# Taking the tiles of a mixture-of-experts layer in pairs, with half-row products of two tiles next to each other

## The reference, cut to what matters

```python
logits = xn2 @ w_gate                                   # 1152 x 8
top_vals, top_idx = jax.lax.top_k(logits, 2)
gates = jax.nn.softmax(top_vals, axis=-1)
...
h = jax.nn.gelu(xn2 @ w1 + bb1, approximate=False)      # 192 -> 768, per expert
return (acc + g[:, None] * (h @ w2 + bb2), None)        # 768 -> 192, weighted by the gate
...
return x + moe_out.reshape(Bx, Nx, C)
```

## Time and profile before

| | us |
|---|---|
| median of 3 runs (lowest, highest) | 360.93 (359.34, 362.2) |
| the profiled execution | 360.52 |
| its span, first to last instruction | 358.7 |
| transposes of tile 4, start | 267.20 |
| transposes of tile 19, start | 340.80 |
| mean granted TensorE clock | 0.974 |

### The profile page before, as it was taken

How to read it: one execution, slowest core, us unless ns; L and a number is a source line. 1 busy time by engine, 2 the same in 40 slices (tenths; PEclk the granted TensorE clock), 3 DMA queues, 4 the chain that set the end, 5 groups by cost and what they waited for, 6 DMA issues and landing times.

```text
span 358.7 us, 7680 instructions
## 1 busy us (share of the span) xinstructions
PE 328.8 (92%) x2651; PEld 284.8 (79%) x2651; DVE 209.2 (58%) x580; ACT 188.9 (53%) x505; POOL 84.3 (24%) x85
## 2 busy tenths in 40 slices
PE   8999997999799899999998888999899999989990
PEld 6977785787588888978997777788798998979890
DVE  1738995698988744453847785885333334332441
ACT  1064516946559177675757786223554455534450
POOL 9410002000000111010001000112164555645642
PEclk9999999899899999999999999996999999999997
DMA  8970000000000594911834222222122333223322
GB/s 268 354 232 0 3 0 1 0 2 0 0 2 0 153 319 122 261 47 48 243 118 108 60 80 92 68 55 76 49 38 43 53 54 54 38 43 55 63 31 25
DMA packets 23698, 29.18 MB, mean 81 GB/s; under 512 B 6010, under 2 KB 18762, under 8 KB 23658
## 3 DMA queue, kind: packets, MB, share of 16 engines
q1 hardware_dynamic: 19770, 23.85, 22.4%
q0 software_dynamic: 3888, 4.81, 8.3%
HBM read 23.54 MB, written 5.11 MB: 80 GB/s over the span
## 4 chain that ended last, share of the span: by engine, by line
PE 44%; DVE 15%; DMA 12%; ACT 12%; issue 11%; POOL 2%; DVEq 1%; POOLq 1%; ACTq 0%
DMA out<-ffn 11%; PE banks L1318 7%; PE banks L1348 7%; PE banks L1319 6%; PE banks L1564 3%; PE banks L1415 3%; PE banks L1547 2%; PE banks L1389 2%; PE banks L1459 2%; PE banks L1390 2%; PE banks L1471 2%; ACT patch L842 1%; POOL rs L635 1%; DVE st L974 1%; ACT xh L718 1%
## 5 line engine op out<-in xcount | busy, mean ns | idle before, releaser
L635 POOL TENSOR_TENSOR rs<-va,consts 96x6 f32<-96x6 f32 (+1 forms) x16 | 17.4, 1087 | 199.5 <-DVE va L980 101.3
L1564 PE MATMUL banks<-arena,ffn 128*128 x240 | 42.9, 329 | 0.0
L667 POOL DMA_INDIRECT out<-ffn x20 | 32.3, 1617 | 44.1 <-DVE ffn L1275 37.4
L1564 PEld LDWEIGHTS banks<-arena,ffn 128*128 128x128 f32 x240 | 38.5, 190 | 0.6 <-issue 0.2
L906 ACT ACTIVATE ffn<-banks,chans 128x128 f32<-128x128 f32 x21 | 9.6, 458 | 52.9 <-PE banks L1537 52.9
L657 POOL DMA_INDIRECT vs<-xh_scratch,ffn x21 | 21.9, 1041 | 17.6 <-DVE ffn L1242 9.3
L1415 PE MATMUL banks<-rvw,ffn 128*96 128x192 f32 x144 | 25.4, 327 | 0.5 <-ACT ffn L814 0.5
L1348 PE MATMUL banks<-arena,patch 128*96 128x192 f32 x144 | 25.0, 327 | 0.0
L1348 PEld LDWEIGHTS banks<-arena,patch 128*96 128x96 f32 x144 | 23.1, 163 | 1.7 <-issue 1.2
L1415 PEld LDWEIGHTS banks<-rvw,ffn 128*96 128x96 f32 x144 | 23.3, 163 | 0.8 <-ACT ffn L814 0.8
L738 ACT ACTIVATE ht<-banks,chans 128x288 f32<-128x288 f32 (+1 forms) x24 | 12.6, 583 | 19.3 <-PE banks L1363 19.2
(11 more groups left out here) (227 smaller groups left out, 766.5 us busy)
## 6 DMA issues: line engine op xcount, KB each, us to landing
arena<-in_w SPq DMA_DIRECT2D x8, 576.0 KB, 7.7
patch<-in_xp SPq DMA_DIRECT2D x12, 288.0 KB, 6.0
arena<-in_w1a SPq DMA_DIRECT2D x8, 384.0 KB, 6.9
vs<-v_scratch SPq DMA_DIRECT2D x24, 114.8 KB
arena<-in_w1b SPq DMA_DIRECT2D x16, 96.0 KB, 5.9
v_scratch<-vt SPq DMA_DIRECT2D x4, 229.5 KB, 2.7
xh_scratch<-xh SPq DMA_DIRECT2D x4, 216.0 KB, 2.4
out<-h SPq DMA_DIRECT2D x1, 864.0 KB, 5.2
```

The source lines that it names most:

```text
L635: pool.tensor_tensor(dst, src, const_("power", T)[:, 0:n * GTILES], ALU.pow).then_inc(rstd_ready, 1)
L667: pool.indirect_dma_start(out[:, :], bass.IndirectOffsetOnAxis(ap=IS[:, j:j + 1], axis=0), YG[j % 2], None, compute_op=ALU.add).then_inc(s ...
L1564: ins = mm(ps[:, 0:C], HST[j % 2][:, 128 * k:128 * (k + 1)], W2[:, bass.ds(e, 1), C * k:C * (k + 1)], start=(k == 0), stop=(k == HB - 1))
```

## The change

Up to tile 16 the tiles are taken in pairs.

- PE: `up(j + 1)` with its halves last, `up(j + 2)` with its halves first (so twelve half-row products follow each other), then `turn_tokens(j + 3)` and `turn_tokens(j + 4)`, then `down(j)` and `down(j + 1)`. The pairs have `j` = 0, 2, ..., 14.
- ACT: `gelu(j + 1)`, `turned(j + 3)`, `turned(j + 4)`, `gelu(j + 2)`.
- DVE: `take_gate(j + 2)`, `weights(j + 3)`, `take_gate(j + 3)`, `weights(j + 4)`, `gated(j)`, `gated(j + 1)`. At the start `weights(2)` comes ahead of the first two `take_gate`.
- POOL: four gathers, then `gather(j + 4)`, `scatter(j)`.
- The PSUM banks follow the new order; the buffers keep their number (three `XG`, two each of `XT`, `WE`, `HST`, `YG`).

```diff
--- before.py
+++ after.py
@@ -38,6 +38,7 @@
 E = 8
 MT = (2 * TOK + E * 127) // 128
 FULL = 2 * TOK // 128
+PAIRED = FULL - 2
 XW = 256 + E
 EPS = 1e-5
 FAR = -1e38
@@ -175,11 +176,14 @@
 
 def moe_jobs():
     out = [("b1",), ("rank",), ("list",)]
-    out += [("xt", 0), ("xt", 1), ("h", 0, 0), ("h", 0, 1)]
-    for j in range(MT):
+    out += [("xt", 0), ("xt", 1), ("h", 0, 0), ("h", 0, 1), ("xt", 2)]
+    for j in range(0, PAIRED, 2):
+        out += [("h", j + 1, 0), ("h", j + 1, 1), ("h", j + 2, 0), ("h", j + 2, 1)]
+        out += [("xt", j + 3), ("xt", j + 4), ("y", j), ("y", j + 1)]
+    for j in range(PAIRED, MT):
         if j + 1 < MT:
             out += [("h", j + 1, 0), ("h", j + 1, 1)]
-        if j + 2 < MT:
+        if PAIRED + 2 < j + 2 < MT:
             out.append(("xt", j + 2))
         out.append(("y", j))
     return out
@@ -667,11 +671,11 @@
                 pool.indirect_dma_start(out[:, :], bass.IndirectOffsetOnAxis(ap=IS[:, j:j + 1], axis=0),
                                         YG[j % 2], None, compute_op=ALU.add).then_inc(scattered, 16)
 
-            for j in range(3):
+            for j in range(4):
                 gather(j)
             for j in range(FULL - 2):
-                if j + 3 <= min(FULL, MT - 1):
-                    gather(j + 3)
+                if j + 4 <= min(FULL, MT - 1):
+                    gather(j + 4)
                 scatter(j)
             n_used = used(pool)
 
@@ -920,10 +924,13 @@
             turned(0)
             turned(1)
             gelu(0)
-            for j in range(1, FULL):
-                if j + 1 < MT:
-                    turned(j + 1)
-                gelu(j)
+            turned(2)
+            for j in range(0, PAIRED, 2):
+                gelu(j + 1)
+                turned(j + 3)
+                turned(j + 4)
+                gelu(j + 2)
+            gelu(PAIRED + 1)
             act.wait_ge(index_ready, 1)
             n_used = used(act)
 
@@ -1250,6 +1257,7 @@
             dve.wait_ge(loaded["w1b"], 32 * E)
             weights(0)
             weights(1)
+            weights(2)
 
             def take_gate(j):
 
@@ -1274,7 +1282,14 @@
                 ps = full(dve, ("y", j))
                 freed(STT(YG[j % 2], ps[:, 0:C], LST[:, MT + j:MT + j + 1], GB, ALU.mult, ALU.add), ("y", j))
 
-            for j in range(FULL):
+            for j in range(0, PAIRED, 2):
+                take_gate(j + 2)
+                weights(j + 3)
+                take_gate(j + 3)
+                weights(j + 4)
+                gated(j)
+                gated(j + 1)
+            for j in range(PAIRED, FULL):
                 if j + 2 <= FULL:
                     take_gate(j + 2)
                 gated(j)
@@ -1536,22 +1551,36 @@
                 pe.transpose(ps[:, 0:128], XG[j % 3][:, 0:128], ident)
                 end(pe.transpose(ps[:, 128:256], XG[j % 3][:, 128:256], ident), ("xt", j))
 
-            def up(j):
+            def up(j, halves_first=False):
                 taken(pe, ("xt", j))
                 if j == 0:
                     pe.wait_ge(index_ready, 1)
                 pe.wait_ge(we_ready, j + 1)
                 we, xt = WE[j % 2], XT[j % 2]
                 ps = [begin(("h", j, i)) for i in range(2)]
-                for m in range(HB):
-                    mm(ps[m // 3][:, 128 * (m % 3):128 * (m % 3 + 1)], we[:, 128 * m:128 * (m + 1)], xt[:, 0, :], start=(m % 3 == 0), stop=False)
-
-                for k in range(3):
-                    for i in range(2):
-                        r = slice(C1 * i, C1 * (i + 1))
-                        ins = mm(ps[i][:, 128 * k:128 * (k + 1)], we[r, HID + 128 * k:HID + 128 * (k + 1)], xt[r, 1, :], start=False, stop=(k == 2))
-                        if k == 2:
-                            end(ins, ("h", j, i))
+
+                def whole(first):
+                    for m in range(HB):
+                        ins = mm(ps[m // 3][:, 128 * (m % 3):128 * (m % 3 + 1)], we[:, 128 * m:128 * (m + 1)], xt[:, 0, :],
+                                 start=first and m % 3 == 0, stop=not first and m % 3 == 2)
+                        if not first and m % 3 == 2:
+                            end(ins, ("h", j, m // 3))
+
+                def halves(first):
+                    for k in range(3):
+                        for i in range(2):
+                            r = slice(C1 * i, C1 * (i + 1))
+                            ins = mm(ps[i][:, 128 * k:128 * (k + 1)], we[r, HID + 128 * k:HID + 128 * (k + 1)], xt[r, 1, :],
+                                     start=first and k == 0, stop=not first and k == 2)
+                            if not first and k == 2:
+                                end(ins, ("h", j, i))
+
+                if halves_first:
+                    halves(True)
+                    whole(False)
+                else:
+                    whole(True)
+                    halves(False)
                 if j < FULL:
                     expert[j] = tile_expert(j)
 
@@ -1569,18 +1598,25 @@
             turn_tokens(0)
             turn_tokens(1)
             up(0)
+            turn_tokens(2)
             n_used = used(pe)
 
             def ahead(j):
 
                 if j + 1 < MT:
                     up(j + 1)
-                if j + 2 < MT:
+                if PAIRED + 2 < j + 2 < MT:
                     turn_tokens(j + 2)
 
-            for j in range(FULL - 1):
-                ahead(j)
+            for j in range(0, PAIRED, 2):
+                up(j + 1)
+                up(j + 2, halves_first=True)
+                turn_tokens(j + 3)
+                turn_tokens(j + 4)
                 down(j)
+                down(j + 1)
+            ahead(PAIRED)
+            down(PAIRED)
 
             def rest(a):
 
```

## The result

The changed kernel takes 424.94 us (median of 4 runs, 424.67 to 427.87) against 361.07 us: ratio 1.179, 95% interval 1.172 to 1.186. It is 64 us slower. The profiled execution took 424.67 us, of which the span is 422.9.

A forecast was written before the change was run, and what follows sets the result against it. PE and a loop through PE, DVE, POOL and the DMA queue were taken as level. Start 264.0, eight loops of 16.12, tail 17.9 and 1.8 outside gave 412.7; 10.4 for the clock gave 423.1, said as 423.5 (405 to 438).

The forecast's parts named there:

- The loop: Expert stage, transposes through down, gelu, bias copy, two scatters and gather: 16.12 us a pair against 9.81 for two tiles.
- The start: First tiles: weights(2) ahead of the first gate delays gather(3) to 259.44; tile 4's transposes come at 264.0, before 267.20.
- The clock: PE's clock falls to 1.2 GHz in each loop's waits: 1.3 us a loop, 10.4 us for eight.
- The half-row products: PE, twelve half-row products in a row: a saving of 0 to 1.8 us, booked at nothing.
- The rest: From tile 19's transposes to the end, hardly changed: 17.9 us.
- The loop without the clock: Rival: transposes between PE's two waits keep the clock up, 413 us; chance 0.2.
- One scatter in the loop: Rival: PE waits only on gather(j+5), the second landing falls outside, 11.7 us a pair, 377 us; chance 0.05.
- The stalls go: Rival: gathers are ready in time, so PE sets the stage's pace; stalls and halves are saved, 354 us; chance 0.04.
- What the profile was to show: Signs in the expert stage: transposes 16 to 18 us apart, scatters in couples, PE idle 6 to 8 us a pair.

The follow-up runs named there:

- pool_order: Changed kernel with POOL issuing the gathers of tiles j+5 and j+6 ahead of scatters j and j+1, DVE's order left as changed: 366.02 us, ratio 1.011 to before.
- dve_order: Changed kernel with weights(j+4) moved behind gated(j) and gated(j+1) on DVE, POOL's order left as changed: 396.94 us, ratio 1.096 to before.
- before_swapped: Kernel before, tiles one by one, with scatter(j) put ahead of gather(j+3) on POOL: 437.55 us, ratio 1.209.
- fillers_half: Changed kernel with 6, 10 or 12 unused filler products on PE ahead of its waits for gathers: 415.51 us, ratio 1.144 to before.
- best_halves_last: Same as best, but up(j+2) with its halves last, so half-row products of two tiles stand apart: 359.09 us, ratio 0.994 to before.
- best: Changed kernel with gathers j+5, j+6 before the pair's scatters, gathers 19, 20 before scatter 14, weights(j+4) behind gated(j+1), first gates before weights(2): 359.27 us.

## Why the prediction was right

Forecast 423.5 us (405 to 438), measured 424.94. The mechanism was right, and the closeness of the figure is in part luck: errors of 1 to 2.4 us cancelled. By its steps:

- *The loop.* 16.12 us at full clock, plus 1.3 for the clock: 17.42; measured 17.37. The first loop (265.07 to 281.10) ran `down` at full clock and took 16.03. Its terms: to gelu 2.50 (2.46 said), gelu 1.66, 0.15, bias copy to scatter 2.10 (2.20), scatter to scatter 4.78 (4.41), 1.89, gather to transposes 2.95 (3.35). Over all eight loops the mechanism is as said, and the closeness of the sum is in part luck: from scatter to scatter it took 4.45 as a mean, from the gather to the transposes 3.05 and not 3.35, 2.4 us less in all, and this hid that the clock cost more than was booked. pool_order and dve_order show that the links are in the loop, before_swapped that the one on POOL acts without the pairs.
- *The start.* Tile 4's transposes at 264.0 said, 265.07 measured. `gather(3)` did move from 254.36 to 260.94 (259.44 said), as `weights(2)` held the first gate; the 1.5 us above the forecast are a slower clock in the first `up`.
- *The clock.* 10.4 us said, about 10 measured with fillers_half. In the trace of the changed kernel gelu started 2.50 us after the transposes in the first loop and 3.75 to 4.54 after them in the other seven, 11.6 us in all. The low clock stood in the loop as said (0.80 is the mean granted in the stage), but in seven loops and at 1.2 to 2.0 us each, not in eight at 1.3. The prediction's 2.2 us of PE work in the loop should be the 2.46 of its own sum, and its upper bound 2.5. What it took from the Trainium skill (TensorE: Matmul & The Clock Gate, section HAM oscillation), that waits on data inside a loop make every round start slow, agrees with these seven rounds.
- *The half-row products, booked at nothing.* Confirmed for the time: the changed kernel waits elsewhere, and best_halves_last equals best. The 24 records together take 1.54 us (288.03 to 289.57) against 2 x 0.87 = 1.74 apart, 0.20 us a pair, within the 0 to 0.22 said. So the effect is there on PE. That a change of tiling mode is its cause was not tried by itself.
- *The rest.* 17.9 us said from tile 19's transposes, 18.9 measured; `down(17)` ran at the low clock (not foreseen).
- *The rivals.* The loop without the clock (413) fell for the change; fillers_half, which holds the clock up, comes near it. One scatter in the loop (377) fell by the couples with a landing between. "The stalls go" fell for the change, but its own mechanism is real: opened on POOL, the loop gives 366 at once. Its price of 354 was too low for pairs (359.3), since it left out the later first scatter and the scatters' landings as a second bound, and nearly right for single tiles (355.7).
- *What the profile was to show:* transposes 16 to 18 us apart (16.0 to 18.5), PE idle 6 to 8 us a pair (5.6 to 6.8), couples of scatters 4.4 apart (4.3 to 4.8), the bias copy waiting for L920, and the clock near 0.8 came. The gap between couples was 12.6 to 13.7, a little above the 11 to 13 said.

## What to carry to other kernels

When steps are reordered on one engine, follow the loop through every in-order queue before counting the engine's own saving: a transfer issued "one tile further ahead" is late if its consumer moved two ahead, and what it stands behind on its queue counts, not its distance in tiles. Sum the loop in both branches, PE's and DVE's, and compare the sum with the busy time of the engine; the larger is the pace. And before pairing work to save an engine's switches, ask whether the next bound, here a chain of scatters that each wait for a landing, leaves room for the saving, and what the pairs cost at the start, where the first result comes later.

## What was not expected of the hardware

- From a scatter to the next that waits for its landing it is 4.2 to 4.6 us mostly (after, best), though the median landing is 3.6, and single ones took 4.8 (after), 6.1 (best), 5.5, 5.9 and 6.3 us (fillers_half).
- One wait of 3.4 us on PE was followed by the low clock (dve_order: L1283 4.25 us after the transposes instead of 2.57); with waits of 0.5 to 1.9 us and fillers ahead of them the stage had 0.99 (fillers_half).
- A filler product of 128 x 192 in float32 is two records and takes 0.33 us at full clock; a count of records is not a count of products.
